# One-hot tiles of the last 17 steps of a graph attention kernel, made on GpSimd instead of ScalarE

## What is computed

```python
xl = (xm @ Wl.T + bl).reshape(n, h, d)
xr = (xm @ Wr.T + br).reshape(n, h, d)
e = (ea_f @ We.T).reshape(-1, h, d)
u = leaky_relu(xl[src_f] + xr[dst_f] + e, 0.2)
logits = jnp.einsum('ehd,hd->eh', u, att)
p = exp(logits - segment_max(logits, dst_f)[dst_f])
alpha = p / segment_sum(p, dst_f)[dst_f]
out = segment_sum(xl[src_f] * alpha[:, :, None], dst_f).reshape(n, h * d) + bias
return x + out @ W_m2n.T
```

## Time and profile before

| | us |
|---|---|
| median of 3 runs | 2251.33 (2247.74 to 2254.03) |
| profiled execution, its own time | 2249.4 |
| its span in the profile | 2247.6 |
| PE busy | 2120.0 (94%) |
| POOL busy | 1599.2 (71%) |
| ACT busy | 1543.5 (69%) |
| DVE busy | 1470.5 (65%) |

### The profile page before, as it was taken

How to read it: one execution, slowest core, us unless ns; L and a number is a source line. 1 busy time by engine, 2 the same in 40 slices (tenths; PEclk the granted TensorE clock), 3 DMA queues, 4 the chain that set the end, 5 groups by cost and what they waited for, 6 DMA issues and landing times. The chain is left out here.

```text
span 2247.6 us, 61841 instructions
## 1 busy us (share of the span) xinstructions
PE 2120.0 (94%) x11843; PEld 1356.6 (60%) x11844; DVE 1470.5 (65%) x4242; ACT 1543.5 (69%) x4421; POOL 1599.2 (71%) x1693
## 2 busy tenths in 40 slices
PE   8499999989999999899999999999999999999887
PEld 7345666656665666566656665666566656666645
DVE  7545666656765666566657665766576656666675
ACT  6346777667776776677767776777677767777733
POOL 6677777777777777777777777777777777777113
PEclk9789999999999999999999999999999989999989
DMA  6344454445444544454445544554444445454127
GB/s 231 92 115 118 119 124 113 118 112 125 116 118 116 125 117 118 113 122 119 117 116 121 120 113 118 121 120 114 118 121 120 112 116 124 117 117 119 43 80 114
DMA packets 309964, 263.67 MB, mean 117 GB/s; under 512 B 172166, under 2 KB 281292, under 8 KB 308782
## 3 DMA queue, kind: packets, MB, share of 16 engines
q1 hardware_dynamic: 251570, 145.37, 25.1%
q0 software_dynamic: 57632, 113.02, 22.3%
q10 hardware_dynamic: 348, 0.82, 0.1%
HBM read 247.57 MB, written 16.89 MB: 118 GB/s over the span
## 5 line engine op out<-in xcount | busy, mean ns | idle before, releaser
L784 POOL DMA_INDIRECT xl_g<-xl_table,src_tab x1612 | 1535.8, 953 | 499.0 <-issue 474.1
L1003 PE MATMUL banks<-msg,onehot 128*128 128x177 f32 x3416 | 644.5, 332 | 4.5 <-ACT msg L1058 4.0
L1003 PEld LDWEIGHTS banks<-msg,onehot 128*128 128x128 f32 x3416 | 529.1, 194 | 168.3 <-issue 141.5
L1150 DVE SCALAR_TENSOR_TENSOR uT<-banks,uT 128x512 f32<-128x512 f32 x427 | 295.1, 691 | 500.3 <-ACT uT L1065 495.0
L1027 ACT ACTIVATE xl_z<-xl_g 128x256 f32 x854 | 309.9, 408 | 364.9 <-DMA xl_g<-xl_table,src_tab 291.1
L1049 ACT ACTIVATE distance<-iota_n,minus_slot 128x128 f32<-128x128 f32 x1708 | 539.2, 386 | 0.0
L958 PE MATMUL banks<-attrT,Wc_br 33*128 33x512 f32 x854 | 490.1, 654 | 0.0
L954 PE MATMUL banks<-onehotT,xr_parts 128*128 128x256 bf16 x2562 | 359.4, 277 | 58.4 <-DVE onehotT L1106 43.4
L962 PEld LDWEIGHTS banks<-ident,xl_z 128*128 128x128 f32 x1708 | 181.9, 142 | 331.9 <-issue 273.6
L1128 DVE TENSOR_TENSOR msg<-xl_g,banks 128x256 f32<-128x256 f32 x854 | 320.3, 415 | 71.7 <-PE banks L1003 55.4
L1065 ACT ACTIVATE uT<-banks 128x512 f32<-128x512 f32 x427 | 250.4, 586 | 132.9 <-PE banks L962 131.6
(11 more groups left out here) (193 smaller groups left out, 1312.0 us busy)
## 6 DMA issues: line engine op xcount, KB each, us to landing
slot_bc<-slot_dram SPq DMA_DIRECT2D x427, 128.0 KB
attrT<-in_attr_cols SPq DMA_DIRECT2D x854, 32.0 KB
rbf<-in_attr_rows SPq DMA_DIRECT2D x854, 32.0 KB
xl_g<-xl_table,src_tab POOLq DMA_INDIRECT x1612
masks<-masks_dram SPq DMA_DIRECT2D x108, 96.5 KB
out<-in_x SPq DMA_DIRECT2D x16, 336.0 KB
out<-xl_g POOLq DMA_DIRECT2D x6, 896.0 KB, 8.6
xl_g<-xl_table SPq DMA_DIRECT2D x7, 448.0 KB, 6.6
```

The source lines that it names most:

```text
L784: pool.indirect_dma_start(out=xl_g[:, g % PRING, i], out_offset=None, in_=xl_table, in_offset=bass.IndirectOffsetOnAxis(ap=src_tab[:, j:j ...
L1003: mm = nc.tensor.matmul(U_ps[j % 2][:, h], onehot[:, j % 2, t], msg[:, j % 2, t], start=i == 0, stop=i == PT - 1)
L1150: nc.vector.scalar_tensor_tensor(out=uT[:, s % URING], in0=z_ps[s % 2], scalar=SLOPE, in1=uT[:, s % URING], op0=ALU.mult, op1=ALU.add).the ...
```

## The change

For steps 410 (`DRAINED`) to 426, GpSimd makes the one-hot tiles once its gathers are done, one operation a tile: (node number - slot) compared with 0. ScalarE no longer makes them there; its copy of the attributes gets the wait for `agg_done` that its one-hot pass had carried. The counter `oh_ready` now rises by 4 (`TILES`) a step instead of 3 (`TICK`), one for each of GpSimd's operations, in all 427 steps and for all who wait for it.

```diff
--- before.py
+++ after.py
@@ -58,6 +58,7 @@
 FLIGHT = 8
 FREES = FREE_ROW * -(-PIECES // (FREED * FREE_ROW))
 TICK = 3
+DRAINED = STEPS - LAG + 1
 ROWS = BATCH * HEADS
 SEQ = 2 * SPLIT * BATCH + 1
 MASK = PIECE + 1
@@ -937,6 +938,12 @@
             for j in range(GATHERS - FLIGHT, GATHERS):
                 pool.wait_ge(landings[j % FLIGHT], 16 * (j // FLIGHT + 1))
                 pool.sem_inc(landed, 1)
+            pool.wait_ge(oh_ready, TILES * DRAINED)
+            for m in range(DRAINED, STEPS):
+                pool.wait_ge(agg_done, m - 1)
+                for t in range(TILES):
+                    nc.gpsimd.tensor_scalar(onehot[:, m % 2, t], iota_n[:], minus_slot[:, TILES * m + t:TILES * m + t + 1],
+                                            0.0, ALU.add, ALU.is_equal).then_inc(oh_ready, 1)
 
         @block.tensor
         def _(pe):
@@ -994,7 +1001,7 @@
                     j = s - LAG
                     pe.wait_ge(msg_ready, TICK * (k - LAG + 1))
                     pe.wait_ge(attr_ready, TICK * (k - LAG + 1))
-                    pe.wait_ge(oh_ready, TICK * (k - LAG + 1))
+                    pe.wait_ge(oh_ready, TILES * (k - LAG + 1))
                     if inside(k - LAG - 2, STEPS):
                         pe.wait_ge(added, TICK * (k - LAG - 1))
                     for h in range(SPLIT):
@@ -1042,9 +1049,9 @@
                     else:
                         nc.scalar.activation(factor[:], factor_ps, ACT.Copy).then_inc(factor_ready, 1)
                 m = s - LAG + 1
-                if inside(k - LAG + 1, STEPS):
-                    if inside(k - LAG, STEPS):
-                        act.wait_ge(oh_ready, TICK * (k - LAG + 1))
+                if inside(k - LAG + 1, DRAINED):
+                    if inside(k - LAG, DRAINED):
+                        act.wait_ge(oh_ready, TILES * (k - LAG + 1))
                     for t in range(TILES):
                         nc.scalar.activation(distance[:, t], iota_n[:], ACT.Abs,
                                              bias=minus_slot[:, one(TILES * (k - LAG + 1) + t)]).then_inc(dist_ready, 1)
@@ -1052,8 +1059,10 @@
                     if inside(k - LAG - 1, STEPS):
                         act.wait_ge(agg_done, k - LAG)
                     nc.scalar.activation(onehot[:, m % 2], distance[:], ACT.Relu, scale=-1.0, bias=1.0
-                                         ).then_inc(oh_ready, TICK)
+                                         ).then_inc(oh_ready, TILES)
                 if inside(k - LAG + 1, STEPS):
+                    if isinstance(k, int) and k - LAG + 1 >= DRAINED:
+                        act.wait_ge(agg_done, k - LAG)
                     act.wait_ge(loads[m % ARING], (r * (UNROLL // ARING) + (s - LAG + 1) // ARING + 1) * FULL)
                     nc.scalar.activation(msg[:, m % 2, :, CNT:AGG],
                                          rbf[:, m % ARING].rearrange("p (t k) -> p t k", t=TILES), ACT.Copy
```

## The result

| | kernel before | changed kernel |
|---|---|---|
| median, 8 runs each | 2253.02 us | 2258.51 us |
| range | 2247.74 to 2258.72 | 2255.36 to 2260.26 |
| profiled execution | 2249.4 | 2260.3 |

The range of the kernel before is of seven of its eight runs; the eighth was a disturbed one, of 2396.86 us, and the median of the seven is 2252.00. The ratio is 1.0027, with a 95% interval from 1.0014 to 1.0040: the change costs 3 to 9 us. That is a loss, small but real, and it lies outside the range that was forecast. It lies just inside the 0.3% that the forecast took for what a measurement can tell; with eight runs on each side the measurement told it.

A forecast was written before the change was run, and what follows sets the result against it. PE's work and POOL's gathers bound the looped turns, DVE's batch chain the drain. ACT's relief gave -1.3 us, all other terms 0, so the median 2251.33 became 2250.0 us; range 2246.0 to 2254.5.

The forecast's parts named there:

- the one for wrong: Signs of failure: longer looped turn, DVE waiting for POOL or longer DVE instructions, or drain idle of PE put down to POOL.
- What bounds the kernel, and the loop: Looped turns: PE's work and POOL's gathers set the pace, not ACT; PE busy 976 of 1000 us.
- the counter's step of 4: Looped turns: one register instruction more on PE, one less on ACT, covered by the sequencer's lead; 0 us.
- The rival on PE's register instruction: Looped turns: without a sequencer lead each grows by 0.1 us, giving 2288 us; chance 5%.
- the one on ACT's pace: Loop: ACT was pacing it, so losing a register instruction saves 17.7 us, giving 2232 us; chance 4%.
- GpSimd makes 68 tiles: Drain: 0.35 us a tile, 1.4 us a step, hidden behind DVE's release of PE; 0 us.
- The rival "GpSimd becomes the bound of the drain": Drain: a tile over 0.77 us makes GpSimd the bound, +6.8 us, 2258 us; chance 3%.
- ACT's relief, -1.3 us: End of the drain: PE's last sums no longer wait for ACT and start earlier, ending the loop 1.3 us sooner.
- `attr_ready`, 0 us: ACT's attribute copy now waits itself for the sums of two steps before, shorter than anything beside it; 0 us.
- DVE and GpSimd hold each other: Drain: 17 DVE instructions may start a tile late, at most 9.5 us, likelier 1 us (2251); chance 5%.
- TensorE's clock: Drain: same clock fall expected; one more or one less at a later wait is 1.5 us either way.

The follow-up runs named there:

- e3: Kernel before with two value-preserving masks on register values, only the counter's step 4 instead of 3: ratio 1.0007 to the kernel before, drain 49.9 us.
- e2: The whole change on the base of e1, so with the same masks: ratio 1.0062 to the kernel before, drain 54.2 us.
- e1: Control: kernel before plus two masks on register values that change no value: ratio 1.0034 to the kernel before, drain 50.2 us.
- e10: Changed kernel with the masks, on the chip of e9: ratio 0.9998 to the kernel before, drain 54.7 us.
- e9: Control again, kernel before plus the masks, on another chip than e1: ratio 1.0002 to the kernel before, drain 50.1 us.
- e11: Changed kernel with masks, mult in place of the comparison on GpSimd (0.372 us a tile): ratio 0.9982 to the kernel before, drain 50.2 us.
- e6: Changed kernel with masks, each GpSimd tile made by a single comparison (0.601 us): ratio 1.0013 to the kernel before, drain 51.0 us.
- e5: Changed kernel with masks, GpSimd making only one of four tiles a step, the other three left out: ratio 1.0008 to the kernel before, drain 49.7 us.
- e7: Changed kernel with masks, GpSimd making tiles 0 and 1 and ACT tiles 2 and 3: ratio 1.0011 to the kernel before, drain 49.6 us.
- e4: Kernel of e1 plus eight trial operations on GpSimd behind its gathers, beside a busy DVE: tile's form 729 ns, drain 48.4 us.
- e8: Kernel before with masks plus 21 trial operations on GpSimd after the loop's last add: tile's form 715 ns, drain 49.1 us.
- e12: Control once more, kernel before plus the masks, on a further chip: ratio 1.0067 to the kernel before, drain 50.6 us, finale 94.9 us.

## Why the prediction was wrong, step by step

Of the forecast's own signs the one for wrong came: in the drain PE's idle time is put down to POOL, and the 68 instructions take 0.717 us, above the 0.56 at most that would have shown it right.

**What bounds the kernel, and the loop.** Right. PE's busy time in 1000 to 2000 us is again 976, positions along the loop show no trend, and the counter's step of 4 costs nothing that shows (e3: 1.0007, where 38 us would have been 1.012). The rival on PE's register instruction falls with it, and so does the one on ACT's pace, since the loop became no shorter.

**GpSimd makes 68 tiles: the step that failed.** It read: a tile 0.35 us, between 0.288 and 0.558, a step 1.4 us, hidden. Measured: 0.717 us and 2.8 to 2.9 us a step. The term was 0; in the drain the loss is 4.0 us (e2 against e1), 4.6 (e10 against e9) and 6.5 (the two profiled executions), where the ratio gives 6.1 (3 to 9) for the whole kernel. Split by what PE did, its idle time in the drain rose by 3.7, 3.0 and 3.8 us, and its busy time, on the same matmuls, by 0.3, 1.6 and 2.7 us, the more the lower the mean clock was. The idle part is the waiting for GpSimd; whether that also brings on the lower clock isn't shown. With 0.372 us instead, and nothing else changed, the drain is as long as without the change (e11). The way of working was at fault too: I took the bounds from L402, which looked nearest in kind because it had two operations, and from a cast, and left out L387, which stood in the same list of groups with a mean of 1078 ns. Halved for half the columns it gives 0.54 us, and with all of it fixed 1.08; such a range reaches over the 0.77 us at which I had put the turn, and the rival could not have had 3%. (A slip beside it: no gain, a microsecond of holding and the highest run of before make 2255.0 and not the 2254.5 of the forecast's upper end. The measured 2258.51 is above both.) The upper bound should have been the dearest row of that engine and opcode, not the one that resembles.

The Trainium skill, in "GPSIMD Engine Reference", section "3.1 Elementwise — side-by-side cycle accounting", gives 1.03 cycles an element for bodies of up to two operations. By that 128 columns take an estimated 0.11 us at 1.2 GHz besides the dispatch, 0.9 ns a column. The trace agrees for the addition and multiplication (0.9 ns, from 442 and 558) and disagrees for the comparison, at 3.3 ns a column (715 and 502); the measurement decides, and only the second was in this change.

**The rival "GpSimd becomes the bound of the drain"** is what happened. That its time, 2258, is also what came (2258.51) is in part luck: the median of the kernel before came out 1.7 us above the one that the forecast started from, and the rival's 6.8 us were reckoned for a tile of 0.77 us. Its point of decision was too high. I had set the sum of all tiles against the length of the drain, as if GpSimd could work through. It can't: with two buffers it may begin a step only when the sums of two steps before are done, so where the batch's chain on DVE holds everybody, GpSimd stands as well (3.55 us in the changed kernel) and can't catch up afterwards. At 0.601 us PE still waited 3.3 us for it (e6), at 0.372 not at all (e11): with four tiles a step the turn lies between these, not at 0.77.

**ACT's relief, -1.3 us.** The mechanism and the place were right and the size too large. From the start of the sums of step 422 to that of step 426 the timelines give 10.1 us in the kernel before, 10.0 in e9, 9.4 in e5 and e11, and 9.3 in e7: 0.6 to 0.8 us, all at the end of the drain. The terms that were missing stand in e5's lines above. I had let DVE go from its adds to the next messages in 0.03 us and in no time at all; it took 0.26 (2150.76 to 2151.02) and 0.28 (2153.05, the end of its rescale, to 2153.33), with nothing to wait for by the profile, and e7 has the same two gaps. I had read them in the earlier trace rows as waits for PE. The rest of that sum held: 2.03 and 1.62 us between, as forecast. In e11 the 0.6 us at the end were lost again before step 422, and its drain is no shorter than the control's; DVE's longer instructions are a likely reason, not a shown one. The kernels with ACT's tiles scatter from 48.4 to 50.6 us among themselves, the short ones (e3, e4, e8) at a mean clock above 0.90, so half a microsecond in a whole drain is rough in any case.

**`attr_ready`, 0 us.** Nothing speaks against it: the waits of PE that the profiles of e5 and e11 put down to the copy L1067 (1.3 us each) are waits for DVE's adds, as said under e5.

**DVE and GpSimd hold each other.** True, and small: DVE's busy time in the drain rose from 37.44 to 37.97 us (37.46 to 38.07 in e9 and e10), half a microsecond, where I had 1 for the likelier price; the most, 38.65, was in e6. The messages and adds kept their means (418, 330 and 340 ns) and so did the scan L1175 (704); what grew is L1209 (297 to 347) and the small copy L1173 (156 to 294), which like L1209 has its input in SBUF. GpSimd's tiles lost nothing to speak of, with a median of 717 ns beside DVE and 715 alone.

**TensorE's clock.** I forecast "one fall more or less, 1.5 us". In the drain it makes up nearly all of the loss's spread, by PE's busy time above: the mean clock was 0.85 in the changed kernel's profiled drain (56.7 us), 0.88 in e10 (54.7) and 0.91 in e2 (54.2). In the finale it moved by more, see below.

## What to carry to other kernels

Price a new instruction from the trace by opcode and form, and take as the upper bound the dearest row of that engine and opcode per element, even if it does less arithmetic; here an addition alone on GpSimd cost 602 ns and an addition with a multiplication 371. An engine that is idle in a stretch isn't free capacity if its work is tied to buffers that the stretch's chain frees: it has only the time between two hand-overs, and 2.8 us of tiles did not fit where the others needed 2.1. A wait's name in a profile is an inference: ask which step the named instruction belongs to, since here several waits of PE were put down to a copy of the next step. And when ACT's work is worth 0.6 us in the place from which it is taken, the best that can come of moving it is below what these totals can tell.

## What the runs showed of the hardware beyond that

The finale, whose code no variant touches, took 88.3 to 94.9 us (e8 with its trials left out), and 89.6 and 94.9 in two executions of one kernel (e9, e12). The longer ones, e6, e7 and e12, have a stretch of some 15 us in which the clock stays at half while PE is busy almost throughout; e7's, for the same place as above:

```profile
2177.13:2192.13 15.00, 14.31 (x32) 6.64 (x32) 9.04 (x15) 1.01 (x1) 5.23 (x2) 0.51 0.00 0
```

What decides whether the clock comes back early was not found. It moves the end by 3.6 to 5.3 us, as much as the change under study: a single execution of this kernel can't judge an effect of that size.
